# A graph network's relation passes: one gather for each tile of edges, with staging by ScalarE, in place of one gather for each step

## The chip, the cores and the metric

The kernel runs on one core of a Trainium2 chip. The metric is the device time of one execution in microseconds (us). Before the change it was 3381.78 us, the median of three runs (3381.7, 3381.78 and 3384.83 us).

## The reference

Four graph networks run one after the other over the same 3125 nodes (128 features) and 100,000 edges, each with a residual and a layer norm. The edges come sorted by destination. The change touches the last one, a relational network with two layers and 8 relations:

```python
def rgcn_layer(x, src, dst, etype, W, W_root, b, num_rels):
    N = x.shape[0]
    h = jnp.einsum('ni,rio->rno', x, W)
    msg = h[etype, src]
    seg = dst * num_rels + etype
    sums = jax.ops.segment_sum(msg, seg, num_segments=N * num_rels)
    cnt = jax.ops.segment_sum(jnp.ones(msg.shape[0], x.dtype), seg, num_segments=N * num_rels)
    mean = sums / jnp.maximum(cnt, 1.0)[:, None]
    agg = mean.reshape(N, num_rels, W.shape[-1]).sum(axis=1)
    return agg + x @ W_root + b

h = jax.nn.relu(rgcn_layer(x, src, dst, edge_type, W1, root1, b1, 8))
y = rgcn_layer(h, src, dst, edge_type, W2, root2, b2, 8)
x = layernorm(x + y)
```

## The kernel before

The instructions are written out by hand for each engine; every engine runs its own list in order and meets the others by semaphores. There is no scheduler, so the order of the code is the order on the engine.

**Tiles, windows and steps.** The 100,000 sorted edges are cut into T = 782 tiles of 128 edges, one edge for each partition. The destinations are cut into windows of 64 nodes (WR = 64), 49 of them. A tile whose edges belong to two windows must be worked on twice, once for each, so a pass over all edges has JR = 782 + 49 - 1 = 830 steps: each step is one (tile, window) pair, and most tiles have one step, 48 of them one more.

**The plan (the first 94 us).** The kernel finds at run time which tile and which window a step has. DVE makes masks (L1162, from what ACT wrote in L786) of the steps that belong to a tile, PE multiplies tables of the edges with the masks (L444), and the result in PSUM is the table for the steps: source, relation, destination, tile. This is done in four chunks of up to 512 steps: two for the adjacency matrix (977 steps with windows of 16 nodes), two for the relation passes (512 and 318 steps). `expand` on DVE (L1080 to L1155) turns each chunk into indices, codes and windows. SP writes those of the relation passes to DRAM (L371 to L373) and reads them back later (L389 to L391). After the plan DVE waits for these writes (L1169) and clears a part of the adjacency matrix (L1170), and the building of that matrix begins (L464 on PE, L1177 on DVE). PE gets leave for it from SP, in a loop over gates that reads its numbers from SBUF into registers, 32 at a time (L377 to L384).

**The adjacency matrix and the three networks before (94 to 1060 us)** are not touched.

**The two relation passes.** Pass 0 (L655, `scatter(0)`) sums rows of `table1`, the node features, pass 1 (L668) rows of `table2`, which the stage between the passes makes. In each of the 830 steps of a pass
- POOL issues one indirect DMA (L739), which gathers 128 rows of 256 half-precision numbers (each value as a high and a low half) into one of NG = 6 buffers `gath`. It waits for the step 6 before to be done on PE (`scattered`);
- DVE makes a one-hot matrix 128x512 of the edges' (node, relation) codes (L1459), 4 steps ahead;
- PE multiplies the one-hot matrix with the gathered rows: 12 matmuls (L584, L587) into one of 3 pairs of PSUM banks. It waits for the gather's semaphore, for the one-hot matrix, and for the pair of banks;
- DVE adds the pair of banks into `sums` at the window of the step, whose number it has in a register (L1475). Every 32 steps it reads 32 windows into registers (L1469).

SP and ACT do nothing in a pass, but for work on weights in pass 0: four squares on ACT at its beginning (L934 to L937), products on PE, reductions on DVE, and three more instructions on ACT (L940 to L945).

**Between the passes** the sums are scaled and go through both layers' weights (25 blocks), POOL clears `sums` block by block (L750), and SP writes `table2`. After pass 1 the slots are scaled and placed (L682), and the last norm follows.

In the profile's rows most tiles of the passes carry the name `adj`: they lie in the space of the adjacency matrix.

## Time and profile before

| | |
|---|---|
| median of 3 runs | 3381.78 us |
| the profiled execution's own time | 3388.58 us |
| its span | 3386.7 us |
| PE busy | 2448.9 us (72%) |
| DVE busy | 2483.4 us (73%) |
| POOL busy | 1985.1 us (59%) |
| ACT busy | 509.9 us (15%) |

The profile is of one execution; its own time is 6.8 us above the median of the runs, and 1.9 us of it lie outside the span. A busy share is an average over stages with different limits, so what counts is which wait ends last in a stage. Of the span, each of the two relation passes takes 1040 us, the stage between them 193 us, the plan 94 us, and the rest, up to pass 0, 966 us.

### The profile page before, as it was taken

How to read it: one execution, taken by the hardware profiler on the slowest of the kernel's cores; microseconds unless marked ns; L12 is line 12 of the kernel's file. 1: busy time of each engine (PE TensorE's matmuls, PEld its weight loads, DVE VectorE, ACT ScalarE, POOL GpSimd, SP SyncE). 2: the span in 40 equal slices, each digit the busy share in tenths (PEclk: the TensorE clock that was granted, in tenths of full speed). 3: DMA queues.
4: the chain of work that ended last, by engine and by line, in shares of the span. 5: the costliest groups of instructions: out<-in, count | busy, mean ns of one | idle time of the engine just before them, and what ended most of it. 6: DMA issues, size and time to landing. Idle time of an engine off the chain costs nothing.

```text
span 3386.7 us, 73088 instructions
## 1 busy us (share of the span) xinstructions
PE 2448.9 (72%) x27967; PEld 1801.3 (53%) x27967; DVE 2483.4 (73%) x6336; ACT 509.9 (15%) x989; POOL 1985.1 (59%) x2158
## 2 busy tenths in 40 slices
PE   4677778998994766666666666996666666676667
PEld 1222255557443555555555555775555555565556
DVE  5999983556416877777777777667777777777777
ACT  2455552116112000000000000550000000000003
POOL 1788840000006777777777776116777777777776
PEclk9889898998997999999999999998999999999999
DMA  1000000000011222222222221112222222222221
GB/s 42 16 1 1 1 6 2 1 1 2 1 39 48 53 54 53 54 54 54 54 54 54 54 54 45 70 76 60 54 53 54 54 53 54 53 54 54 54 54 40
DMA packets 76149, 138.75 MB, mean 41 GB/s; under 512 B 29902, under 2 KB 44640, under 8 KB 75810
## 3 DMA queue, kind: packets, MB, share of 16 engines
q0 software_dynamic: 53120, 108.90, 12.3%
q1 hardware_dynamic: 18934, 24.46, 2.1%
q8 instruction: 231, 3.78, 0.5%
q10 hardware_dynamic: 3756, 0.73, 0.2%
q14 instruction: 108, 0.88, 0.1%
HBM read 116.35 MB, written 17.62 MB: 40 GB/s over the span
## 4 chain that ended last, share of the span: by engine, by line
PE 32%; DMA 25%; POOL 17%; DVE 14%; issue 8%; ACT 2%; ACTq 1%; SPq 0%; DVEq 0%; POOLq 0%
DMA adj<-table,adj 25%; POOL adj L739 17%; PE banks L584 8%; DVE hi_hot L1177 7%; PE banks L516 6%; PE banks L509 3%; PE banks L587 3%; DVE lo_hot L1185 3%; PE banks L631 2%; PE banks L643 2%; PE banks L491 1%; PE banks L682 1%; PE banks L495 1%; ACT adj L822 1%; PE banks L616 1%
## 5 line engine op out<-in xcount | busy, mean ns | idle before, releaser
L584 PE MATMUL banks<-adj 128*128 128x129 f16 x13280 | 1412.9, 226 | 697.7 <-DMA adj<-table,adj 683.8
L739 POOL DMA_INDIRECT adj<-table,adj x1660 | 1574.7, 949 | 538.5 <-PE banks L584 316.2
L584 PEld LDWEIGHTS banks<-adj 128*128 128x128 f16 x13280 | 1077.1, 100 | 924.8 <-DMA adj<-table,adj 910.7
L1475 DVE TENSOR_TENSOR adj<-adj,banks 128x516 f32 x1660 | 1147.4, 691 | 460.6 <-PE banks L584 423.0
L587 PE MATMUL banks<-adj 128*128 128x127 f16 x6640 | 1248.6, 224 | 0.0
L587 PEld LDWEIGHTS banks<-adj 128*128 128x128 f16 x6640 | 672.4, 101 | 1.3 <-issue 1.0
L1459 DVE TENSOR_SCALAR adj<-adj 128x512 f16<-128x512 f16 x1660 | 642.9, 388 | 0.0
L713 POOL TENSOR_SCALAR lo_hot<-minus_iota,zT 128x128 f16<-128x128 f16 x392 | 323.5, 842 | 134.6 <-PE banks L464 72.6
L464 PE MATMUL banks<-hi_hot,lo_hot 128*128 128x400 f16 x977 | 269.6, 383 | 114.6 <-DVE hi_hot L1177 75.2
L1177 DVE TENSOR_SCALAR hi_hot<-iota,zT 128x400 f16<-128x400 f16 x977 | 271.0, 340 | 7.1 <-PE banks L464 6.7
L720 POOL MEMSET adj<- 128x1548 f16 x1 | 1.4, 1388 | 468.2 <-PE banks L516 468.2
L464 PEld LDWEIGHTS banks<-hi_hot,lo_hot 128*128 128x128 f16 x977 | 101.8, 104 | 282.3 <-issue 228.7
L516 PE MATMUL banks<-adj,split 128*128 128x512 f16 (+1 forms) x1190 | 235.7, 356 | 0.0
L996 ACT ACTIVATE adj<-adj 128x128 f32<-128x128 f32 x75 | 22.0, 392 | 1050.2 <-DVE adj L1487 1050.2
L516 PEld LDWEIGHTS banks<-adj,split 128*128 128x128 f16 x1190 | 109.6, 98 | 117.3 <-issue 2.9
L956 ACT ACTIVATE adj<-banks 128x512 f16<-128x512 f32 x50 | 26.9, 585 | 940.3 <-PE banks L616 940.3
L509 PE MATMUL banks<-adj,split 128*128 128x512 f16 (+1 forms) x560 | 115.4, 370 | 25.0 <-DVE split L1268 20.2
L809 ACT ACTIVATE adj<-banks 128x400 f16<-128x400 f32 x196 | 98.7, 503 | 185.1 <-PE banks L464 184.3
L1185 DVE TENSOR_SCALAR lo_hot<-minus_iota,zT 128x128 f16<-128x128 f16 x585 | 119.8, 279 | 0.0
L750 POOL MEMSET adj<- 128x1032 f32 x25 | 24.0, 959 | 153.6 <-PE banks L616 153.6
L509 PEld LDWEIGHTS banks<-adj,split 128*128 128x128 f16 x560 | 53.0, 101 | 86.6 <-issue 20.4
L1315 DVE SCALAR_TENSOR_TENSOR zT<-banks,dinv,rows 128x128 f32<-128x128 f32 x75 | 21.2, 342 | 97.8 <-PE banks L533 97.6
(229 smaller groups left out, 1811.7 us busy)
## 6 DMA issues: line engine op xcount, KB each, us to landing
adj<-table,adj POOLq DMA_INDIRECT x1660
table<-adj SPq DMA_DIRECT2D x25, 512.0 KB, 2.6
table<-split SPq DMA_DIRECT2D x6, 256.0 KB, 2.3
out_dram<-xres SPq DMA_DIRECT2D x6, 256.0 KB
adj<-in_L_gnn_W_dram SPq DMA_DIRECT2D x1, 1024.0 KB, 7.4
adj<-in_L_gnn_W_dram SPq DMA_DIRECT2D x2, 512.0 KB, 9.1
adj<-scr_index SPq DMA_DIRECT2D x1, 830.0 KB
scr_index<-adj SPq DMA_DIRECT2D x1, 512.0 KB
```

The source lines that it names most:

```text
L464: e.matmul(banks[:, bass.ds(c, 1), 0:NC].rearrange("p o n -> p (o n)"), lo_hot[:, g % NLO, j % LG, :], hi_hot[:, j % NHI, :], start=False, ...
L509: e.matmul(bank[c][:, 0:n], split[:, k, s, :], adj[:, k, c0:c0 + n], start=(k == 0 and s == 0), stop=False)
L516: m = e.matmul(bank[c][:, 0:n], split[:, k, s, :], adj[:, k, c0:c0 + n], start=False, stop=(k == NB - 1 and s == 1))
L584: m = e.matmul(ps[:, g * CH // 2:g * CH // 2 + b - a], hot[:, s, g * P:g * P + P], gath[:, s, a:b], start=(q == 0), stop=(q == 1), skip_gr ...
L587: e.matmul(ps[:, g * CH // 2 + D + 1:(g + 1) * CH // 2], hot[:, s, g * P:g * P + P], gath[:, s, 0:CH // 2 - D - 1], start=True, stop=True, ...
L713: e.tensor_scalar(lo_hot[:, g % NLO, k, :], minus_iota[:, :], nlo[:, j:j + 1], None, ALU.is_equal).then_inc(low_pool, 1)
L739: e.indirect_dma_start(gath[:, s, 0:2 * D], None, table, bass.IndirectOffsetOnAxis(ap=index[:, which, j:j + 1].bitcast(U32), axis=0)).then ...
L809: e.activation(adj[:, :, w * WA:(w + 1) * WA], v.rearrange("p (h n) -> p h n", n=WA), ACT.Copy).then_inc(evicted, 1)
L1177: e.tensor_scalar(hi_hot[:, j % NHI, :], iota[:, :], code[:, j:j + 1], None, ALU.is_equal).then_inc(high, 1)
L1185: e.tensor_scalar(lo_hot[:, g % NLO, j % LG, :], minus_iota[:, :], nlo[:, j:j + 1], None, ALU.is_equal).then_inc(low_dve, 1)
L1459: e.tensor_scalar(hot[:, s, :], iota_r[:, :], code_r[:, j:j + 1], None, ALU.is_equal).then_inc(hot_set, 1)
L1475: e.tensor_tensor(a, a, ps[:, :].rearrange("p (g d) -> p g d", g=G)[:, :, 0:D + 1], ALU.add).then_inc(accumulated, 1)
```

## The change

A pass gathers each tile once, 782 gathers, and still has 830 steps. The buffers are now 16 (`gath`, NG = 16) and belong to tiles. A step's rows come to PE by way of a second set of 6 buffers (`edge`), into which ACT copies the tile of the step; which tile that is it reads from a register (`tile_regs`, 32 at a time). SP runs a loop over the tiles in each pass (`relay`): it waits for the gathers in order and counts them in `landed`, for which ACT waits, and it tells POOL (`slot_free`) which buffers are free: those of tiles whose last step ACT has copied, a number that SP too reads into registers (`last_regs`). The one-hot matrices keep 6 buffers. The three instructions on ACT in pass 0 are put between its copies, and DVE's work on the second layer's weights begins 14 steps later.

In the plan, the index tables need only one column for each tile: PE turns the table of edges (35 small matmuls at its beginning), ACT writes them out, and SP sends them to DRAM once. So `expand` for the relation chunks loses three DVE instructions of each chunk and gets a small one (the row of tiles), and PE's product for a tile and chunk has 4 matmuls in place of 6. DVE makes the row of last steps from `ends` (2 small instructions).

POOL fills `place` after pass 0, not before it, and `place` lies in memory of its own.

```diff
+LEAD = 8
-        NG = 6
+        NG, NSTG, NHOT = 16, 6, 6
-        gath = carve([P, NG, D + 1], F16)
-        hot = carve([P, NG, G * P // 2], F16)
+        gath = carve([P, NG, D], F16)
+        edge = carve([P, NSTG, D + 1], F16)
+        hot = carve([P, NHOT, G * P // 2], F16)
-        index = carve([P, 2, JR], I32)
+        index = carve([P, 2, T], I32)
-                   {0: [S_LO, S_HI], 1: [TYPE], 2: [D_LO[1], D_HI[1]], 3: [TILE]})
+                   {1: [TYPE], 2: [D_LO[1], D_HI[1]], 3: [TILE]})
# SP
+            e.wait_ge(index_set, 3)
+            e.dma_start(scr_i, out_i[:, :, :]).then_inc(last_out, 16)
...
+            def relay(which):
+                for t in range(T):
+                    u = t + LEAD - NG
+                    if u >= 0 and t + LEAD < T:
+                        if u % REGS == 0:
+                            n = min(REGS, T - NG - u)
+                            e.load(last_regs[0:n], last_row[:, u:u + n])
+                        e.reg_alu(least, last_regs[u % REGS], 1, ALU.max)
+                        e.wait_ge(staged_edges[which], least)
+                        e.sem_inc(slot_free[which], 1)
+                    e.wait_ge(gathered[t % NG], 16 * (which * (-(-(T - t % NG) // NG)) + t // NG + 1))
+                    e.sem_inc(landed[which], 1)
# PE, at its beginning
+            for b in range(TB):
+                rws = P if b < TFULL else TLAST
+                at = slice(b % 4 * P, b % 4 * P + rws)
+                for q in (S_LO, S_HI):
+                    e.matmul(bank[4 + b // 4][:, at], piece[0:rws, q, b, :], ident16[0:rws, 0:rws],
...
# PE, scatter
-                    e.wait_ge(gathered[s], 16 * uses)
+                    e.wait_ge(staged_edges[which], j + 1)
# POOL
             def gather(which, table):
-                base = which * JR
-                for j in range(JR):
-                    s = j % NG
-                    if base + j >= NG:
-                        e.wait_ge(scattered, base + j - NG + 1 if j >= NG else base)
+                if which:
+                    e.wait_ge(staged_edges[0], JR)
+                for t in range(T):
+                    s = t % NG
+                    if t >= NG:
+                        e.wait_ge(slot_free[which], t - NG + 1)
                     e.indirect_dma_start(
-                        gath[:, s, 0:2 * D], None, table,
-                        bass.IndirectOffsetOnAxis(ap=index[:, which, j:j + 1].bitcast(U32), axis=0)).then_inc(gathered[s], 16)
+                        gath[:, (t + 1) % NG, :], None, table,
+                        bass.IndirectOffsetOnAxis(ap=index[:, which, t:t + 1].bitcast(U32), axis=0)).then_inc(gathered[s], 16)
# ACT
+            def stage_edges(which):
+                base = which * JR
+                for j in range(JR):
+                    if j % REGS == 0:
+                        n = min(REGS, JR - j)
+                        e.load(tile_regs[0:n], tile_row[:, j:j + n])
+                    e.reg_alu(least, tile_regs[j % REGS], 1, ALU.max)
+                    e.wait_ge(landed[which], least)
+                    if base + j >= NSTG:
+                        e.wait_ge(scattered, base + j - NSTG + 1)
+                    c = e.snap(tile_regs[j % REGS], min_val=1, max_val=T) % NG
+                    e.activation(edge[:, j % NSTG, 0:2 * D], gath[:, bass.ds(c, 1), :].rearrange("p o f -> p (o f)"),
+                                 ACT.Copy).then_inc(staged_edges[which], 1)
+                    if which == 0 and j >= REGS:
+                        between(j - REGS)
# DVE, expand for a relation chunk
-                    e.tensor_copy(out_i[:, 0, 0:n], sets[0][:, 0:n]).then_inc(own_dve, 1)
-                    e.tensor_copy(Y, sets[1][:, 0:n]).then_inc(own_dve, 1)
...
-                    e.scalar_tensor_tensor(out=out_i[:, 1, 0:n], in0=sets[0][:, 0:n], scalar=float(REL), in1=Y,
-                                           op0=ALU.mult, op1=ALU.add).then_inc(sums_read, 1)
+                    e.tensor_scalar(rows_i[:, 1, 0:n], sets[3][0:1, 0:n], 1.0, None, ALU.add).then_inc(own_dve, 1)
```

How the instructions move. POOL's list from the sums' clearing to the end of pass 1, before (`table` is the gathered table, `adj 128x25800` the clearing of `sums`):

```order
L731 MEMSET adj 128x25800
L739 DMA adj<-table,adj 128x256 [waits table1_out,rel_set,list_in]
L739 DMA adj<-table,adj 128x256 x5
L739 DMA adj<-table,adj 128x256 [waits scattered] x824
L750 MEMSET adj 128x1032 [waits row_turned] x25
L739 DMA adj<-table,adj 128x256 [waits scattered,table2_out1,table2_out0]
L739 DMA adj<-table,adj 128x256 [waits scattered] x829
```

and now:

```order
L778 MEMSET adj 128x25800
L787 DMA adj<-table,adj 128x256 [waits table1_out,rel_set,list_in]
L787 DMA adj<-table,adj 128x256 x15
L787 DMA adj<-table,adj 128x256 [waits slot_free0] x766
L798 MEMSET adj 128x1032 [waits row_turned] x25
L800 MEMSET place 128x1024
L804 COPY place<-ident 64x4x64 [waits own_pool]
L804 COPY place<-ident 64x4x64 [waits place_set] x3
L787 DMA adj<-table,adj 128x256 [waits table2_out1,staged_edges0,table2_out0,place_set]
L787 DMA adj<-table,adj 128x256 x15
L787 DMA adj<-table,adj 128x256 [waits slot_free1] x766
```

A pass has 782 gathers in place of 830; what they wait for comes from SP, and `place` is filled between the passes.

ACT's list at the beginning of pass 0, before (the squares, the three instructions on bounds and weights, then the first block between the passes):

```order
L934 ACTIVATE zT<-adj 128x2304 [waits table1_out,l3_in]
L935 ACTIVATE h<-colp 128x2
L936 ACTIVATE zT<-adj 128x256
L937 ACTIVATE w1p<-adj 128x2048
L940 ACTIVATE bound<-bound 128x4 [waits bound_set]
L942 ACTIVATE w1p<-adj,scales 128x2304 [waits scale_set]
L945 ACTIVATE adj<-adj,scales 128x2304 [waits w_low]
L956 ACTIVATE adj<-banks 128x8x64 [waits row_turned,w_low]
```

and now:

```order
L1024 ACTIVATE zT<-adj 128x2304 [waits table1_out,l3_in]
L1025 ACTIVATE h32<-colp 128x2
L1026 ACTIVATE zT<-adj 128x256
L1027 ACTIVATE w1p<-adj 128x2048
L999 TENSOR_LOAD rows [waits list_in]
L1000 REGISTER_ALU
L1004 ISA [waits landed0]
L1005 ACTIVATE adj<-adj 128x256
L1000 REGISTER_ALU
L1004 ISA [waits landed0]
L1005 ACTIVATE adj<-adj 128x256
```

A step on ACT is three instructions, a register's maximum, one that takes the buffer's number and carries the wait, and the copy of 128x256; a load of registers stands ahead of every 32 steps.

DVE's list for the first relation chunk (512 steps) in the plan, before:

```order
L1097 SCALAR_TENSOR_TENSOR adj<-adj 128x512 [waits own_dve]
L1139 CAST adj<-banks 128x512
L1141 COPY adj<-banks 128x512
L1144 SCALAR_TENSOR_TENSOR adj<-banks,adj 128x512 [waits own_dve]
L1148 SCALAR_TENSOR_TENSOR adj<-banks,adj 128x512 [waits own_dve]
L1151 SCALAR_TENSOR_TENSOR adj<-adj 128x512 [waits own_dve]
L1153 TENSOR_SCALAR adj<-adj 128x512 [waits own_dve]
L1155 CAST adj<-adj 1x512
L1162 TENSOR_SCALAR adj<-adj 128x318 [waits picked_abs] x2
```

and now:

```order
L1188 SCALAR_TENSOR_TENSOR adj<-adj 128x512 [waits own_dve]
L1230 TENSOR_SCALAR adj<-banks 1x512
L1232 SCALAR_TENSOR_TENSOR adj<-banks,adj 128x512
L1236 SCALAR_TENSOR_TENSOR adj<-adj 128x512 [waits sums_read,own_dve]
L1238 TENSOR_SCALAR adj<-adj 128x512 [waits own_dve]
L1240 CAST adj<-adj 1x512
L1247 TENSOR_SCALAR adj<-adj 128x318 [waits picked_abs] x2
```

Three instructions on 128 partitions are gone, one on a single partition is new.

## Rows read from the trace of the kernel before

**Rows 1.** Busy time by stage; columns are named in the first row.

```profile
core 0: us, PE busy (x) PEld busy (x) DVE busy (x) ACT busy (x) POOL busy (x), PEclk, DMA share, GB/s
1060.49:2100.69 1040.20, 703.80 (x9966) 584.65 (x9966) 815.08 (x1700) 8.13 (x7) 787.40 (x830) 0.98 0.21 54
2100.69:2293.47 192.78, 181.18 (x2049) 143.94 (x2049) 122.78 (x207) 91.41 (x200) 23.96 (x25) 0.98 0.18 70
2293.47:3333.56 1040.09, 713.00 (x9936) 604.45 (x9936) 809.56 (x1658) 0.00 (x0) 787.31 (x830) 0.95 0.21 54
```

**Rows 2.** Waits on POOL: waiter, releaser, us in total, times, longest.

```profile
POOL adj L739 <- PE banks L584: 316.2, 1037, 0.3
POOL adj L739 <- issue: 189.4, 621, 0.3
```

**Rows 3.** POOL in order of time: start, us, what, idle before.

```profile
1019.22 1.77 POOL L727 COPY adj<-ident 64x256 f32<-64x256 f32 x4
...
1060.49 1.30 POOL L739 DMA_INDIRECT adj<-table,adj  x1 [17.70 <-DMA table<-split]
...
2099.69 1.00 POOL L739 DMA_INDIRECT adj<-table,adj  x1 [0.30 <-PE banks L584]
...
2277.25 0.96 POOL L750 MEMSET adj<- 128x1032 f32 x1 [6.09 <-PE banks L616]
2293.47 1.71 POOL L739 DMA_INDIRECT adj<-table,adj  x1 [15.26 <-DMA table<-adj]
```

**Rows 4.** One line of code each: ns min/median/max, first and last start.

```profile
L739 POOL DMA_INDIRECT adj<-table,adj x1660: 941/947/1712, 1060.5 to 3332.6; - x185
L1459 DVE TENSOR_SCALAR adj<-adj x1660: 336/349/598, 1057.9 to 3331.9; 128x512 f16<-128x512 f16 x185
L971 ACT ACTIVATE hTp<-h x25: 416/416/417, 2117.8 to 2284.2; 128x256 f16<-128x256 f32 x25
```

**Rows 5.** PE, its first matmul of pass 0, in order of time.

```profile
1063.38 0.29 PE L584 MATMUL banks<-adj 128*128 128x129 f16 x1 [29.87 <-DMA adj<-table,adj]
```

**Rows 6.** The chain that ended last: the longest landing in it.

```profile
2900.57 4.39 DMA adj<-table,adj
```

**Rows 7.** DVE behind a late landing, in order of time.

```profile
3328.56 0.69 DVE L1475 TENSOR_TENSOR adj<-adj,banks 128x516 f32 x1 [1.43 <-PE banks L584]
...
3329.47 0.69 DVE L1475 TENSOR_TENSOR adj<-adj,banks 128x516 f32 x1
```

**Rows 8.** DVE at step 32 of pass 0, where it loads 32 registers.

```profile
1105.63 0.69 DVE L1475 TENSOR_TENSOR adj<-adj,banks 128x516 f32 x1 [1.45 <-issue]
```

**Rows 9.** ACT in the plan, in order of time.

```profile
74.16 0.56 ACT L786 ACTIVATE adj<-adj 128x318 f16<-128x318 f16 x1 [6.27 <-PE banks L444]
76.83 0.56 ACT L786 ACTIVATE adj<-adj 128x318 f16<-128x318 f16 x1 [2.11 <-PE banks L444]
```

**Rows 10.** DVE in the plan, the relation chunks, in order of time.

```profile
79.90 0.68 DVE L1139 CAST adj<-banks 128x512 int32<-128x512 f32 x1
80.50 0.68 DVE L1141 COPY adj<-banks 128x512 f32<-128x512 f32 x1
...
83.35 0.41 DVE L1155 CAST adj<-adj 1x512 int32<-1x512 f32 x1
...
87.65 0.49 DVE L1139 CAST adj<-banks 128x318 int32<-128x318 f32 x1
...
93.83 0.72 DVE L1170 MEMSET adj<- 128x800 uint32 x1 [3.52 <-DMA scr_windows<-adj]
```

**Rows 11.** PE in the plan, its last product and the first of the next stage.

```profile
84.03 1.90 PE L444 MATMUL banks<-adj 128*128 128x318 f16 x12 [1.52 <-DVE adj L1162]
99.32 1.18 PE L464 MATMUL banks<-hi_hot,lo_hot 128*128 128x400 f16 x3 [13.39 <-SPq L383]
```

**Rows 12.** SP's last write of the plan.

```profile
91.55 0.32 SPq L373 DMA_DIRECT2D scr_windows<-adj  x1
```

**Rows 13.** The last add of pass 0 on DVE.

```profile
2103.98 0.69 DVE L1475 TENSOR_TENSOR adj<-adj,banks 128x516 f32 x1 [1.22 <-PE banks L584]
```

More of the change, by code:

```diff
@@ L402, in _ @@
                             split[:, q0:q1, :, :].rearrange("p b q d -> p b (q d)")).then_inc(table1_out, 16)
+            last_regs = [e.alloc_register(f"last_use{i}") for i in range(REGS)]
+            def relay(which):
[10 more added lines that the diff above has]
+                    e.sem_inc(landed[which], 1)
+            e.wait_ge(list_in, 80)
+            relay(0)
             for nb in range(NB):
@@ L930, in _, with between @@
                 split_high(xres, quad, FX)
+            tile_regs = [e.alloc_register(f"tile{i}") for i in range(REGS)]
+            def stage_edges(which):
[13 more added lines that the diff above has]
+                        between(j - REGS)
+            def between(t):
+                if t == 34:
+                    e.wait_ge(bound_set, 6)
+                    e.activation(bound[:, 12:16], bound[:, 8:12], ACT.Sqrt).then_inc(bound_root, 1)
+                elif t == 38:
+                    e.wait_ge(scale_set, 1)
+                    e.activation(w1p[:, 0, :, :].rearrange("p r o -> p (r o)"), w1[:, :], ACT.Identity,
+                                 scale=scales[:, 0, 0:1]).then_inc(w_high, 1)
+                elif t == 54:
+                    e.wait_ge(w_low, RR)
+                    e.activation(w2p[:, 0, :, :, :], w2_r[:, :, :, :], ACT.Identity, scale=scales[:, 0, 2:3]).then_inc(w_high, 1)
             e.wait_ge(l3_in, 16 * (3 + HB))
```

123 lines of the change are left out of this document (77 added, 46 removed).

## The prediction

> **What bounds the kernel now.** I read the busy time by stage first, then the waits of the engine whose instructions fill the passes, then that engine in order of time. By stage [rows 1] the two relation passes are 1040.20 and 1040.09 us, 61% of the span. In them no engine is full: DVE is busy 78%, POOL 76%, PE 68%. The chain of waits there goes back and forth between landings, POOL and PE, and names no bound. The waits on POOL do [rows 2]: 1658 of its 1660 gathers are preceded by an idle of at most 0.3 us, whoever is named as its releaser. So POOL never waits for a buffer; it issues a gather, takes 0.30 us, and issues the next. The gather itself is 947 ns in the median [rows 4]. Over a pass that is 1040.15 / 830 = 1.2532 us for each gather, first start to last end [rows 1, 3]. POOL's rate of issue is the bound, and everything behind it (landing, PE, DVE) follows with slack: when a landing is late, DVE's next add comes 0.91 us after the one before [rows 7], which is what a step costs DVE if nothing is missing.
>
> **Fewer gathers.** A pass issues 782 in place of 830, so 2 x 48 x 1.2532 = **-120.3 us**, if POOL still never waits and a gather costs the same. Both must be shown for the new cover.
>
> *Does POOL wait for SP?* Gather t waits for SP's round t - 8, which begins once tile t - 9 has landed. From the end of gather t - 9 to the start of gather t there are 8 x 1.25 + 0.30 = 10.3 us. A landing takes 1.6 us (first gather's end 1061.79 to the first matmul at 1063.38) [rows 3, 5] and at the worst in the chain 4.4 us [rows 6]. So SP and the copies behind have 5.9 to 8.7 us before POOL stands still. A round also waits for the last step of tile t - 16, which lies a further 8 tiles back.
>
> *Do the steps keep up?* They must now do 830 steps in 782 x 1.2532 = 980 us, 1.181 us each. DVE: 830 x 0.91 = 755 us if no mask is ever long, and at most the 815 us that it was busy in pass 0, weights included [rows 1]; with 26 loads of registers at 1.45 us [rows 8], at most 853 us. ACT: a copy of 128x256 is 416 ns [rows 4]; the nearest dearer row, 128x318 with a bias, is 560 ns [rows 9]. The two register instructions ahead of it I bound by DVE's, which fit with two computing instructions into 0.91 us; so a step is 0.42 to 0.91 us, I take 0.6, and with the loads ACT needs 540 us of 980. ACT's two large weight instructions fall between copies, but ACT was busy 8.1 us in all in pass 0 [rows 1], and the steps catch up 0.2 us a step. PE was busy 704 of 1040 us. SP's round is four semaphore operations and a register operation; by the same DVE row it is under 0.91 us. None reaches 980, so POOL stays the bound, and DVE, at 853, is next.
>
> *A rule against it.* The row first: the gather's duration has 941 ns as its least and 947 as its median, while the mask on DVE goes from 336 to 598 ns [rows 4]; where the two meet, it is DVE that becomes longer. The Trainium skill (SBUF — State Buffer, Who interferes with whom and the box on the trap that DVE blocks DMA) says that a DVE copy or tensor-scalar instruction in a two-port mode locks out POOL, which then cannot write its descriptors until the instruction ends. By that rule the denser masks would stretch each gather (the first rival below); by the row they do not. I go by the row.
>
> **The plan.** PE's product for a tile of the first relation chunk loses 2 of 6 matmuls. ACT's masks follow it 2.67 us apart [rows 9], so the last two that DVE waits for come 2 x 2.67 / 3 = 1.8 us sooner. DVE loses three instructions at 0.60 us and gets one like the 0.34 us of a single-partition row (83.35 to 83.69, start to start; 0.41 alone): -1.5 [rows 10]. The 318-step chunk: PE 12 matmuls in 1.90 us become 8, -0.6 [rows 11]; DVE three at about 0.4, one more at 0.3, -0.9. Two small instructions of DVE before the masks, at most 0.41 each [rows 10], cost about 0.4. Sum **-4.4 us**. PE's 35 matmuls and ACT's two writes are done while DVE still prepares the masks (PE has no other work before DVE's first masks, by the program's order); should they not be hidden, they cost a few us. The other end: DVE waits 3.52 us for the last write [rows 10], which is shorter now without the indices, so down to -8; upwards 0, if PE is bound by something else there.
>
> **Ends of the passes.** After the last gather's end (2100.69) the last add is over at 2104.67 [rows 3, 13], 4.0 us. Now a hop over SP and a copy lie in between: 0.42 for the copy and I take 0.4 for the semaphores, **+1.6 us** for both passes. Bounds: 0.8, and by the longest answer of SP that any row shows (its last write ends at 91.87, PE's gate opens at 99.32, 7.4 us [rows 11, 12]) about 16.
>
> **At nothing.** The squares on ACT (part of its 8.1 us) delay the first copies, not POOL, which has 16 free buffers, 20 us. Filling `place` costs POOL a memset of about 1 us and 1.77 us of copies [rows 3], now after the last clearing at 2277.25; the gather behind it waits until 2293.47 for `table2`, so 15.3 us hide it. Before pass 0 POOL was waiting 17.7 us anyway, so nothing is gained there. SP's writes of the indices go out while SP is idle.
>
> **Sum.** -120.3 - 4.4 + 1.6 = -123.1 us. Against the profiled execution's 3388.58 us that is 3265.5; against the median of the runs, 6.8 us lower, 3258.7. I predict **3259 us**.
>
> **Rivals.**
>
> *The mask lock.* If POOL stands still while a mask is made, a gather contains the mask's time today, and with 830/782 masks for each gather it grows by 0.349 x 48/782 = 0.021 us [rows 4]. 1564 x 0.021 = 34: **3293 us**. For it: the rule. Against: the gather's constant duration [rows 4]. 8%.
>
> *The step, not the gather, carries the 1.253 us* (the change doesn't give what it says): the new chain of SP, ACT, PE and back through buffers takes as long for a step as a gather does now. Then both passes stay at 1040 us: 3381.8 - 4.4 + 1.6 = **3379 us**. Against: the 0.91 us [rows 7] and 6 buffers on each side. 5%.
>
> *Slower: loads of registers stop the relay.* SP and ACT now each load 32 registers every 32 tiles or steps, and during SP's load no landing is told on. DVE's load costs 1.45 us [rows 8]; the only row with SP's is the 7.4 us before the first gate [rows 11, 12], which held one load. If SP's and ACT's both cost 7.4 us and follow each other, that is 14.9 us of standstill in 32 tiles, beyond POOL's slack; with their 34 steps at DVE's 815 / 830 = 0.98 us, 32 tiles take 14.9 + 33.3 = 48.2 us, a pass (24.4 such stretches) 1177 us, and the kernel 3381.8 - 2.8 + 2 x 137 = **3653 us**. It makes the kernel slower from a standstill of 1040.15 / 24.4 - 33.3 = 9.3 us in 32 tiles; a load of 7.4 us alone would nearly be hidden (40.7 us where POOL needs 40.1). For: the relay is a single chain. Against: DVE was at its clearing until 94.55 there [rows 10] and made PE's next masks after it, so much of the 7.4 us need not be SP's. 6%, with milder forms of it in between at 3270 to 3320 us, 3%.
>
> **How the numbers follow.** The forecast has 78%, with its own range 3248 to 3272 (the plan's 0 to -8, the ends' bounds, 0.2% for the runs). A time within 0.2% of before (6.8 us) can't be told from no change. Faster: 78 + 8 + 3 = 0.89. Same: 0.05. Slower: 0.06. The range 3245 to 3300 takes in the lock.
>
> **What the profile after would show.** Right: 782 gathers in a pass, idle 0.30 us before nearly each, first start to last end 980 us; 830 copies on ACT of about 0.42 us; DVE busy about 83% of a pass; the plan's clearing on DVE at about 89.5 instead of 93.83 us; the stage between the passes still 193 us. Wrong: gathers longer than 0.95 us in the median (the lock); idle before gathers released by SP (the relay), in bursts every 32 tiles (the loads); steps at a regular 1.25 us with ACT or PE full. The forecast would also fall if TensorE's granted clock, 0.98 and 0.95 in the passes [rows 1], sank for long: at the lower of its two levels, 1.2 GHz, the 12 matmuls of a step with 128 columns each are 1.28 us, more than the 1.18 us there are.

## The result, and the profile after

The changed kernel takes 3261.51 us (median of 4 runs, 3260.66 to 3262.88) against 3382.28 us (4 runs, 3381.7 to 3384.83) for the kernel before on the same chip: ratio 0.9642, 95% interval 0.963 to 0.9653. Predicted were 3259 us, with 3245 to 3300 as the range. The profiled execution's own time is 3260.66 us, its span 3258.8 us, 127.9 us less than before. The medians differ by 120.8 us; the traced execution of before was 6.3 us above its median, so some of the 127.9 us below are not the change's.

Busy time by stage, after. The stages are the plan (from DVE's first cast to its clearing), the untouched part, pass 0, the stage between, and pass 1; rows two to four answer to [rows 1].

```profile
core 0: us, PE busy (x) PEld busy (x) DVE busy (x) ACT busy (x) POOL busy (x), PEclk, DMA share, GB/s
1052.01:2033.19 981.18, 690.58 (x9948) 594.49 (x9949) 792.79 (x1698) 339.00 (x835) 743.04 (x782) 0.97 0.19 54
2033.19:2224.38 191.19, 180.13 (x2069) 143.20 (x2067) 124.61 (x210) 92.24 (x202) 26.44 (x30) 0.97 0.17 70
2224.38:3205.15 980.77, 679.89 (x9930) 579.96 (x9931) 784.14 (x1658) 332.70 (x828) 742.64 (x782) 0.98 0.19 54
24.37:87.34 62.97, 36.12 (x168) 16.84 (x168) 45.69 (x109) 23.47 (x38) 8.89 (x12) 0.88 0.06 20
87.34:1052.01 964.67, 774.74 (x5531) 413.89 (x5531) 643.12 (x2505) 357.75 (x650) 340.08 (x385) 0.91 0.02 7
```

Both passes lost 59 us and still run at POOL's rate: 981.18 / 782 = 1.2547 and 980.77 / 782 = 1.2542 us for each gather, where it was 1.2532. The waits of the engines, after (waiter, releaser, us in total, times, longest):

```profile
POOL adj L787 <- issue: 443.6, 1455, 0.3
POOL adj L787 <- SPq L436: 32.6, 107, 0.3
ACT adj L1005 <- SPq L438: 1005.1, 1048, 7.1
ACT adj L1005 <- PE banks L637: 236.2, 238, 2.4
ACT adj L1005 <- issue: 50.3, 71, 0.9
PE banks L637 <- ACT adj L1005: 585.8, 908, 30.4
```

1562 of the 1564 gathers start after at most 0.3 us of idle, whoever is named, as in [rows 2]. ACT waits for SP to report a landing and PE for ACT: the relay waits for gathers, not gathers for the relay. One line of code each (ns min/median/max), against [rows 4]:

```profile
L787 POOL DMA_INDIRECT adj<-table,adj x1564: 941/947/1296, 1052.0 to 3204.2; - x196
L1005 ACT ACTIVATE adj<-adj x1660: 398/417/420, 1055.4 to 3207.6; 128x256 f16 x185
L1545 DVE TENSOR_SCALAR adj<-adj x1660: 334/349/593, 1049.4 to 3203.9; 128x512 f16<-128x512 f16 x185
L433 SPq TENSOR_LOAD <-rows x48: 1860/1864/2077, 1063.7 to 3159.0; - x48
L999 ACTq TENSOR_LOAD <-rows x52: 1945/1964/2200, 1051.3 to 3170.4; - x52
```

The last two are the loads of 32 registers on SP and on ACT: 1.86 and 1.96 us each.

The span's difference, piece by piece (start of one row to start or end of another, in both traces):

| piece | before | after | difference | predicted |
|---|---|---|---|---|
| to DVE's first cast (waits for inputs) | 26.03 | 24.37 | -1.66 | 0 |
| first cast to the plan's clearing | 67.80 | 62.97 | -4.83 | -4.4 |
| clearing to first gather | 966.66 | 964.67 | -1.99 | 0 |
| pass 0 | 1040.20 | 981.18 | -59.02 | -60.2 |
| between the passes | 192.78 | 191.19 | -1.59 | +0.8 |
| pass 1 | 1040.09 | 980.77 | -59.32 | -60.2 |
| after the last gather | 53.14 | 53.65 | +0.51 | +0.8 |

### The profile page after: what moved, and what is told of

Its sections match the earlier page's. It is cut to its first block, busy times and chain, and to the rows that moved or that the text cites. A ratio compares the mean times of both kernels' runs of the same rounds, so it can differ in the third digit from the quotient of the medians.

```text
span 3258.8 us, 84381 instructions
## 1 busy us (share of the span) xinstructions
PE 2400.5 (74%) x27974; PEld 1786.4 (55%) x27974; DVE 2433.1 (75%) x6334; ACT 1176.6 (36%) x2651; POOL 1898.6 (58%) x2063
## 3 DMA queue, kind: packets, MB, share of 16 engines
q1 hardware_dynamic: 19354, 24.37, 2.1%
## 4 chain that ended last, share of the span: by engine, by line
POOL 38%; PE 20%; issue 13%; DVE 13%; DMA 8%; SPq 2%; ACT 2%; DVEq 0%; ACTq 0%; POOLq 0%
POOL adj L787 37%; DMA adj<-table,adj 8%; DVE hi_hot L1263 7%; PE banks L571 6%; PE banks L564 4%; DVE lo_hot L1271 3%; PE banks L684 2%; PE banks L696 2%; SPq L433 2%; PE banks L546 1%; POOL lo_hot L767 1%; PE banks L735 1%; PE banks L550 1%; ACT adj L882 1%; PE banks L669 1%
## 5 line engine op out<-in xcount | busy, mean ns | idle before, releaser
L637 PE MATMUL banks<-adj 128*128 128x129 f16 x13280 | 1368.7, 224 | 624.2 <-ACT adj L1005 585.8
L787 POOL DMA_INDIRECT adj<-table,adj x1564 | 1485.7, 950 | 511.9 <-issue 443.6
L640 PE MATMUL banks<-adj 128*128 128x127 f16 x6640 | 1226.6, 222 | 0.0
L1005 ACT ACTIVATE adj<-adj 128x256 f16 x1660 | 665.6, 415 | 1294.1 <-SPq L438 1005.1
L1545 DVE TENSOR_SCALAR adj<-adj 128x512 f16<-128x512 f16 x1660 | 611.7, 369 | 0.0
L872 ACT ACTIVATE banks<-banks 128x400 f32<-128x400 f32 x188 | 91.7, 488 | 6.0
```

What stands on the lines that cost most here:

```text
L637: m = e.matmul(ps[:, g * CH // 2:g * CH // 2 + b - a], hot[:, j % NHOT, g * P:g * P + P], edge[:, j % NSTG, a:b], start=(q == 0), stop=(q ...
L640: e.matmul(ps[:, g * CH // 2 + D + 1:(g + 1) * CH // 2], hot[:, j % NHOT, g * P:g * P + P], edge[:, j % NSTG, 0:CH // 2 - D - 1], start=Tr ...
L787: e.indirect_dma_start(gath[:, (t + 1) % NG, :], None, table, bass.IndirectOffsetOnAxis(ap=index[:, which, t:t + 1].bitcast(U32), axis=0)) ...
L1005: e.activation(edge[:, j % NSTG, 0:2 * D], gath[:, bass.ds(c, 1), :].rearrange("p o f -> p (o f)"), ACT.Copy).then_inc(staged_edges[which], 1)
L1545: e.tensor_scalar(hot[:, s, :], iota_r[:, :], code_r[:, j:j + 1], None, ALU.is_equal).then_inc(hot_set, 1)
```

## The experiments

They ran on four chips, and these are of two kinds. On two of them the kernel before takes 3805.43 and 3803.41 us, not 3382; its stages up to 1060 us are as usual there and only the relation passes are longer. On these ran the runs with fewer gathers (both), short masks, half rows, eight pieces, the changed kernel again, the plan back and the weights moved. The others (four pieces, short loads, eight buffers, SP's increments) ran on two chips like the first one (kernel before 3389.29 us in a single run, and 3391.23 us). A time is compared with a kernel's on the same kind of chip.

**Fewer gathers, nothing else** (kernel before).

```diff
+        def left_out(j):
+            return j % 17 == 16 and j < 816
...
                     s = j % NG
+                    if left_out(j):
+                        continue
                     if base + j >= NG:
...
-                    uses = which * (-(-(JR - s) // NG)) + j // NG + 1
-                    e.wait_ge(gathered[s], 16 * uses)
+                    mine = [i for i in range(s, JR, NG) if not left_out(i)]
+                    uses = which * len(mine) + sum(i <= j for i in mine)
+                    if not left_out(j):
+                        e.wait_ge(gathered[s], 16 * uses)
```

> The kernel before, with 48 of the 830 gathers of each pass left out (every 17th step multiplies whatever rows lie in its buffer, so the sums of those steps are wrong); no relay on SP, no copies on ACT, 6 buffers, 830 steps. Theory (POOL's rate of issue is the bound): a pass has 782 gathers at 1.2532 us, 980 us, and the kernel is 3382.3 - 120.3 = 3262 us. Rival (a step, whatever is gathered for it, carries 1.25 us): both passes stay at 1040 us and the kernel at 3382 us. Its distance to the changed kernel (3261.5 us, with a plan shorter by some 5 us) is what relay and copies cost: under the theory less than 2 us beside the plan.

Measured: 3674.19 us against 3805.43, ratio 0.9652 (0.9636 to 0.9668), -131 us; the passes 1180.48 and 1182.54 us. Run again on another such chip:

> The kernel before, with 48 gathers of each pass left out (the steps 16, 33, 50 and so on use what stands in the buffer); no other edit. Theory (POOL's rate of issue is the bound and nothing else of the change matters): 2 x 48 x 1.253 = 120 us less than before, 3262 us, both passes at 980 us, and idle before the gathers still 0.30 us. Rival (the steps carry part of the time, and the new buffers and copies were needed for the gain): the passes stay above 1000 us, with idle before the gathers released by PE.

Measured: 3671.49 us against 3803.41, ratio 0.9652 (0.9637 to 0.9666); passes 1181.00 and 1179.48 us. On both chips leaving out 48 gathers in a pass takes 66 us from it (1247.62 in the kernel with moved weights, below), 1.4 us each, though POOL does wait there: its waits, second run,

```profile
POOL adj L746 <- PE banks L589: 476.4, 447, 1.8
POOL adj L746 <- issue: 334.1, 1062, 2.8
```

POOL waits for PE here, and the passes stay above 1000 us, which were the rival's signs; so on this chip the run doesn't show that POOL's rate of issue is the bound. Nor does a step have a price of its own: with the same 830 steps the pass became shorter, and it is 1247.62 / 830 = 1.503 us for each gather with all gathers and 1181.00 / 782 = 1.510 with fewer. Late landings don't hold up PE there. In the kernel with moved weights (830 gathers, same kind of chip, below) PE waits 48.0 us for them in both passes, 30.2 of it for the first one, where it waited 683.8 us in the trace of before:

```profile
PE banks L585 <- DMA adj<-table,adj: 48.0, 17, 30.2
```

What the run does show is that fewer gathers shorten the passes without the new buffers and copies. 3262 us could not be tested on this chip.

**Masks of 2 columns in place of 512** (changed kernel; the one-hot matrices keep old contents).

```diff
-                e.tensor_scalar(hot[:, s, :], iota_r[:, :], code_r[:, j:j + 1], None, ALU.is_equal).then_inc(hot_set, 1)
+                n = G * P if base + j < NHOT else 2
+                e.tensor_scalar(hot[:, s, 0:n], iota_r[:, 0:n], code_r[:, j:j + 1], None, ALU.is_equal).then_inc(hot_set, 1)
```

> The changed kernel with DVE's mask made whole only for the first 6 steps; from then on the instruction writes 2 of its 512 columns, so PE multiplies old masks (wrong sums). Theory: the gather's duration does not depend on DVE's masks, it stays at 947 ns in the median, a pass at 981 us and the kernel at 3260 us. Rival (a mask on DVE holds up POOL's descriptors and a gather contains its 0.35 us): gathers fall towards 0.6 us and a pass towards 830 x 0.75 us, the rate of PE and DVE's adds, the kernel below 3000 us.

Measured: 3903.01 us, passes 1288.01 and 1283.73 us; this is the slower kind of chip, so only the durations of single instructions answer. The groups of the two lines (busy us, mean ns | idle before):

```profile
L787 POOL DMA_INDIRECT adj<-table,adj x1564 | 1476.6, 944 | 1131.0 <-SPq L436 719.2 <-issue 376.0 <-DMA table<-split 23.0
L1546 DVE TENSOR_SCALAR adj<-adj 128x2 f16<-128x2 f16 x1654 | 378.3, 229 | 0.0
```

The changed kernel has 359 and 956 ns on such a chip (below). The mask fell by 130 ns; if a gather held a mask's time, it would have fallen by as much, and it fell by 12, or by 4 against fewer gathers, which has whole masks and 948 ns. The lock isn't what a gather's time consists of. That the pass would fall with it couldn't be seen here, as POOL waits for SP.

**Half of each row** (256 bytes for each partition in place of 512; the low halves are not gathered).

```diff
-                        gath[:, (t + 1) % NG, :], None, table,
+                        gath[:, (t + 1) % NG, 0:D], None, table.rearrange("n (h d) -> (n h) d", h=2),
```

> The changed kernel with 256 bytes gathered for each row in place of 512, from wrong places (the index is not doubled), so the sums are wrong. Theory: a gather costs POOL by its 128 rows, not its bytes: 947 ns, a pass 981 us, 3261 us. Rival (the gather's bytes or the transfer are the bound): a gather's time falls with the bytes, to 0.5 to 0.7 us, and DVE becomes the bound at about 850 us a pass, 3000 us.

Measured: 3904.15 us on the same chip, passes 1282.01 and 1281.15 us, gathers 954 ns in the mean (changed kernel below: 1285.29, 1270.69, 956). Half the bytes change nothing, neither in the gather nor in the pass: POOL's 0.95 us are for issuing, not for moving.

**ACT's copy in eight pieces, then in four** (changed kernel; the four differ only in the numbers).

```diff
-                    e.activation(edge[:, j % NSTG, 0:2 * D], gath[:, bass.ds(c, 1), :].rearrange("p o f -> p (o f)"),
-                                 ACT.Copy).then_inc(staged_edges[which], 1)
+                    for q in range(8):
+                        m = e.activation(edge[:, j % NSTG, q * 32:q * 32 + 32],
+                                         gath[:, bass.ds(c, 1), q * 32:q * 32 + 32].rearrange("p o f -> p (o f)"),
+                                         ACT.Copy)
+                    m.then_inc(staged_edges[which], 1)
```

> The changed kernel with ACT's copy of 256 columns cut into 8 instructions of 32 columns. Nothing is left out. Two copies of ACT follow each other 0.30 us apart in the trace of the changed kernel; 8 short ones should take 1.2 to 2.0 us with the step's register work. Theory: a step's work on ACT is free up to 1.18 us and binds beyond it: at 1.6 us a pass is 830 x 1.6 = 1330 us and the kernel 3960 us, POOL idle before its gathers and released by SP. Rival (ACT's copies are never on the path, only landings are): 3261 us.

Measured: 4015.38 us, passes 1344.54 and 1340.29 us, where the changed kernel has 1285.29 and 1270.69 on such a chip (below): 59 and 70 us more. The pieces overlap: ACT was busy 936.37 us of pass 0, 1.13 us a step, not the 1.6 us that the expectation took, so its 1330 us for a pass was met by luck, on a chip where the pass has 1285 us without the pieces.

> The changed kernel with ACT's copy of 256 columns cut into 4 instructions of 64 columns, which should take ACT 0.8 to 1.0 us a step in place of 0.42. Nothing is left out. Theory (a step has 1.18 us, and ACT's work is beside the path): the two passes stay at 981 us, but for some 0.4 us more at the end of each; 3262 us. Rival (the copy is a link of the chain that sets the pace of a step): 0.5 us more for each of 1660 steps, 4090 us.

Measured, on a chip like the first: 3259.82 us (one run), passes 978.90 and 977.72 us. Pass 0 with four pieces, and POOL's waits:

```profile
1054.52:2033.42 978.90, 693.49 (x9954) 598.97 (x9954) 795.24 (x1698) 567.87 (x3319) 740.87 (x782) 0.96 0.22 55
```

```profile
POOL adj L787 <- issue: 442.2, 1451, 0.3
POOL adj L787 <- SPq L436: 33.8, 111, 0.3
```

ACT's busy time in a pass grew by 229 us and the pass by nothing. So the copy was hidden, as forecast, with at least that much to spare on this kind of chip.

**Registers 8 at a time**, on SP and ACT, in place of 32 (changed kernel).

```diff
+SHORT = 8
-                        if u % REGS == 0:
-                            n = min(REGS, T - NG - u)
+                        if u % SHORT == 0:
+                            n = min(SHORT, T - NG - u)
...
-                    if j % REGS == 0:
-                        n = min(REGS, JR - j)
+                    if j % SHORT == 0:
+                        n = min(SHORT, JR - j)
```

> The changed kernel with registers loaded 8 at a time instead of 32, by SP's relay and by ACT: 4 times as many loads, 98 and 104 a pass. Nothing is left out. Theory: a load stops relay or copies by about 1.4 us as on DVE, POOL's slack of 6 to 9 us covers each, and 8 tiles take 10.0 us where the steps need 8.3 us and the loads 1.4 or twice that: 3262 us, at most 3330 us if both loads add up. Rival (the loads are of the 7.4 us kind): 8 tiles would take 16 us, over 4000 us.

Measured: 3266.95 us (one run), passes 984.05 and 984.08 us. Four times as many loads bring 3 us to a pass. But a load of 8 registers is shorter, 0.52 us on SP, so that SP's loads grew only from 24 x 1.86 = 45 us to 96 x 0.52 = 50 us in a pass; the run tests more stops, not longer ones. SP's loads, ACT's waits and POOL's, here:

```profile
L434 SPq TENSOR_LOAD <-rows x192: 520/523/736, 1063.2 to 3194.9; - x192
ACT adj L1006 <- issue: 180.7, 241, 0.9
POOL adj L788 <- issue: 452.9, 1486, 0.3
POOL adj L788 <- SPq L437: 23.2, 76, 0.3
```

ACT's idle that is released by nothing rises from 50.3 to 180.7 us, yet POOL still waits 0.3 us at most. What lengthened the passes is the mean of a gather, 954 ns in place of 950 (1564 x 0.004 = 6 us in all), which also lies among the other runs' 944 to 956. The slower rival's standstill is not there, and its 7.4 us a load are refuted by the loads' own rows (1.86 and 1.96 us for 32 registers, above).

**8 buffers with a lead of 4** in place of 16 and 8 (changed kernel).

```diff
-LEAD = 8
+LEAD = 4
-        NG, NSTG, NHOT = 16, 6, 6
+        NG, NSTG, NHOT = 8, 6, 6
```

> The changed kernel with 8 buffers for tiles in place of 16, and SP's answer 4 tiles ahead in place of 8. Nothing is left out. Theory: POOL's slack for a late landing falls from 5.9 us to 0.9 us and for an ordinary one to 3.7 us, so POOL waits rarely: 3261 to 3275 us, idle before gathers of more than 0.3 us only behind late landings or loads. Rival (16 buffers are what made the gain): the passes lose most of it, 3300 to 3380 us.

Measured: 3267.26 us (one run), passes 983.98 and 982.63 us, gathers 953 ns, POOL's longest idle 0.3 us. Half the buffers would do on this chip.

**The changed kernel again.**

> The changed kernel once more, beside the others of this job, as the measure for them. If the first measurement holds on this chip, 3261 us against 3382 us (ratio 0.964), with 981 us for each pass. The rival for the chip on which the first four experiments ran: if this one's kernel before is at 3805 us again, the changed kernel shows by how much a program with more instructions (84,381 in place of 73,088) suffers there; a slow supply of instructions would put it near 3900 us and over 1.28 us for each gather, although a gather lasts 0.95 us.

Measured: 3893.04 us (5 runs, 3886.61 to 3897.22) against 3803.41 us (15 runs): ratio 1.0236, interval 1.0222 to 1.025. **On this chip the change makes the kernel slower.** By stage (the two passes), the kernel with moved weights (830 gathers) first, fewer gathers next, the changed kernel last:

```profile
1058.25:2305.87 1247.62, 804.15 (x9946) 683.60 (x9947) 831.18 (x1695) 8.13 (x7) 790.30 (x830) 0.89 0.17 45
2498.16:3744.69 1246.53, 794.62 (x9917) 677.37 (x9918) 818.99 (x1653) 0.00 (x0) 790.93 (x830) 0.89 0.17 45
```

```profile
1060.42:2241.42 1181.00, 790.56 (x9950) 673.79 (x9950) 824.68 (x1696) 8.13 (x7) 741.25 (x782) 0.89 0.17 45
```

```profile
1056.27:2341.56 1285.29, 815.62 (x9761) 713.17 (x9762) 767.63 (x1663) 315.30 (x821) 747.85 (x782) 0.84 0.16 41
2549.36:3820.05 1270.69, 809.42 (x9720) 710.58 (x9720) 758.98 (x1619) 310.92 (x813) 747.61 (x782) 0.83 0.16 42
```

Waits of the changed kernel there:

```profile
POOL adj L787 <- SPq L436: 689.7, 498, 5.1
ACT adj L1005 <- PE banks L637: 1516.2, 895, 4.6
PEld banks L637 <- issue: 584.5, 896, 16.9
```

The gather is as cheap as ever (956 ns in the mean), but POOL waits 690 us for SP, SP for ACT, ACT for PE. So the chain through the steps sets the pace, 1285.29 / 830 = 1.55 us for a step. PE's rows in order of time show how a step comes late there:

```profile
1502.24 0.22 PE L637 MATMUL banks<-adj 128*128 128x129 f16 x1 [1.62 <-issue]
...
1505.15 0.22 PE L637 MATMUL banks<-adj 128*128 128x129 f16 x1 [2.06 <-ACT adj L1005]
...
1507.04 0.42 PE L637 MATMUL banks<-adj 128*128 128x128 f16 x2
```

In these rows PE idles 1.6 and 2.1 us between two steps, the first time with no releaser; behind the second stop, from 1506.3 to 1509.7 us, the granted clock is at its lower level (1.2 GHz), and two matmuls take 0.42 us where they take 0.28 at the upper (2.4 GHz). The mean over the pass is 0.84 in place of 0.97. Against fewer gathers alone the changed kernel pays 104 + 91 us in the passes, and 13 + 17 us where it must still work off the tiles that POOL is ahead (207.8 us between the passes in place of 194.7, 71.2 us behind the last gather in place of 54.2); 4 us come back in the plan and the stage behind it. Together 221 us, which turn -132 into +90.

The beginning of a pass shows the stops at their plainest. While POOL fills its free buffers, one gather every 1.25 us, the others nearly stand still. The first three rows of PE are the last matmuls of one step, which wait for no semaphore; the fourth begins the next step and waits for an add of DVE's, whose products PE had finished before 1064 us:

```profile
1069.80 0.27 PE L637 MATMUL banks<-adj 128*128 128x129 f16 x1 [1.89 <-issue]
1071.21 0.27 PE L640 MATMUL banks<-adj 128*128 128x127 f16 x1 [1.14 <-issue]
1072.60 0.27 PE L637 MATMUL banks<-adj 128*128 128x128 f16 x1 [1.12 <-issue]
...
1088.97 0.27 PE L637 MATMUL banks<-adj 128*128 128x129 f16 x1 [16.10 <-DVE adj L1561]
```

```profile
1084.14 0.95 POOL L787 DMA_INDIRECT adj<-table,adj  x1 [0.30 <-issue]
1087.54 0.94 POOL L787 DMA_INDIRECT adj<-table,adj  x1 [2.46 <-SPq L436]
1088.13 0.69 DVE L1561 TENSOR_TENSOR adj<-adj,banks 128x516 f32 x1 [20.77 <-remote]
1088.21 0.42 ACT L1005 ACTIVATE adj<-adj 128x256 f16 x1 [19.58 <-remote]
```

DVE, ACT and PE go on within 0.9 us of each other, 3 us after POOL's last gather in the row has ended at 1085.09.

From one add on DVE to the next it is 21.7 us here, with 16 gathers in it, and 17 to 22 us at the beginning of each pass in all five traces of the changed kernel and its variants on these chips. On the first kind of chip the longest such distance there is 3.5 us, and in the kernel before, where POOL can be only 6 gathers ahead, 4.3 us on these chips. Together with the constant 1.50 to 1.51 us for each gather above, this suggests, and doesn't prove, that on these chips the other engines are held up while POOL issues gathers, and the longer, the further POOL may run ahead. It was not tested: the run with 8 buffers was on a chip where nothing stops.

**The sources' tables back in the plan** (changed kernel).

```diff
-                    {1: [TYPE], 2: [D_LO[1], D_HI[1]], 3: [TILE]})
+                    {0: [S_LO, S_HI], 1: [TYPE], 2: [D_LO[1], D_HI[1]], 3: [TILE]})
...
+                    e.tensor_copy(Y, sets[0][:, 0:n]).then_inc(own_dve, 1)
+                    own.up()
+                    e.wait_ge(own_dve, own.n)
+                    e.tensor_copy(Y, sets[1][:, 0:n]).then_inc(own_dve, 1)
+                    own.up()
                     e.tensor_scalar(rows_i[:, 1, 0:n], sets[3][0:1, 0:n], 1.0, None, ALU.add).then_inc(own_dve, 1)
+                    own.up()
+                    e.wait_ge(own_dve, own.n)
+                    e.scalar_tensor_tensor(out=GE, in0=sets[0][:, 0:n], scalar=float(REL), in1=Y,
+                                           op0=ALU.mult, op1=ALU.add).then_inc(own_dve, 1)
```

> The changed kernel with the sources' tables back in the plan: PE makes 6 matmuls for each tile and relation chunk in place of 4, and DVE again does the three instructions on 128 partitions of each chunk (their result is not used). Theory of the prediction: the clearing on DVE, 62.97 us after its first cast now, comes 4.4 to 4.8 us later, at 67.4 to 67.8, and the kernel takes 4 to 5 us more than the changed one, near 3265.5 us. Rival (DVE's wait for the last write, 2.30 us now, takes up what is added, or ACT's masks set the pace): under 2 us.

Measured: first cast to clearing 26.37 to 95.26, 68.89 us, where the changed kernel beside it has 26.45 to 90.52, 64.07: +4.82 us. The time is 3899.41 us against 3893.04, +6.4, which its runs' spread (3886.88 to 3901.82) can't tell from less. The second chunk with the instructions back, PE's product and DVE, in order of time; last PE's product in the changed kernel:

```profile
84.40 3.47 PE L499 MATMUL banks<-adj 128*128 128x318 f16 x12 [4.19 <-DVE adj L1256]
87.91 0.49 DVE L1179 SCALAR_TENSOR_TENSOR adj<-adj,banks 128x318 f32<-128x318 f32 x1 [3.35 <-PE banks L499]
...
95.26 0.72 DVE L1265 MEMSET adj<- 128x800 uint32 x1 [2.30 <-issue]
```

```profile
80.03 1.36 PE L499 MATMUL banks<-adj 128*128 128x318 f16 x8 [1.02 <-DVE adj L1247]
```

The wait ahead of the clearing is 2.30 us with and without them, so it takes up nothing. But the 4.82 us are not the forecast's terms put back. DVE's two chunks take 2.04 and 1.43 us more, the second product makes DVE wait 2.1 us more, and DVE begins the first chunk 0.8 us sooner than in the changed kernel beside it. The granted clock is part of that: the second product ran at 0.50 here and its 12 matmuls took 3.47 us, where the same 12 took 1.90 at 1.00 in the trace of before [rows 11], and the first ran at 1.00 (42 matmuls in 7.04 us; 11.13 at 0.62 before).

**The weights moved by 8 bytes** (kernel before).

```diff
+        carve([P, 2])
         w1 = carve([P, RR * H])
```

> The kernel before, with its two tables of weights w1 and w2 moved on by 8 bytes in each partition, so that they begin at a multiple of 32 bytes as in the changed kernel; nothing else. Between the passes the changed kernel needs 6.93 us for a block in place of 7.05, though none of its instructions there are changed. Theory (the addresses are the cause): 6.93 us a block, 190 us between the passes in place of 193, the kernel 3 us shorter, 3379 us. Rival (the cause is another, as the clock or what else is in memory): 7.05 us a block as before, no change of the time.

Measured: 3800.05 us against 3803.41, ratio 0.9994 (0.9985 to 1.0003), which settles nothing by itself; but 192.29 us between the passes, where fewer gathers has 194.68 on this chip, and a block in 6.93 us in place of 7.05. One group of PE's in a block (54 matmuls, their moving operand in the memory of `w2`), first of the kernel before, then moved:

```profile
2244.81 3.30 PE L631 MATMUL banks<-adj,w1p 128*128 128x128 f16 x54
```

```profile
2346.31 3.18 PE L632 MATMUL banks<-adj,w1p 128*128 128x128 f16 x54
```

On the moved weights' own chip the group takes 3.30 us in fewer gathers, so the chip is not what differs. 0.12 us for 54 matmuls is the whole difference of a block, and 25 blocks make 3.0 us (2.4 in the stage as a whole). The addresses are the cause.

**4100 semaphore increments on SP in pass 0** (kernel before).

```diff
+            e.wait_ge(gathered[0], 16)
+            for i in range(4100):
+                e.sem_inc(gate, 1)
             for nb in range(NB):
```

> The kernel before, with 4100 semaphore increments that nobody waits for on SP, begun when the first gather of pass 0 has landed; pass 1 is left as it is and serves as the measure. It asks what the mere number of instructions costs that the changed kernel gives to SP and ACT. Theory A (the engines' instructions come over something that they share, and it is this supply that runs short on the chip on which the kernel before takes 3805 us): on that chip the changed kernel has about 5600 more instructions in a pass and pays 290 - 200 = 90 to 105 us more for pauses, 16 to 19 ns each, so 4100 of them cost 65 to 80 us and pass 0 takes 1312 to 1325 us where pass 1 takes 1247; on a chip on which the kernel before takes 3382 us nothing, as the changed kernel there has no pauses: 1040 us for both. Theory B (what matters is which instructions they are, ACT's copies and the chain through them, not their number): both passes alike on either chip, 1247 or 1040 us, and the kernel's time that of before within 0.2%.

Measured, on a chip like the first: 3391.37 us against 3391.23, ratio 1.0001 (0.9991 to 1.0011); passes 1041.52 and 1040.42 us. There the number of instructions costs nothing, as both theories have it; the chip on which they differ was not met again.

## Why the prediction was right

*The bound.* POOL's rate of issue, from 830 gathers at 1.2532 us: the changed passes are 782 gathers at 1.2547. Of the predicted -120.3 us came -118.3; the 1.3 ns that a gather takes more in the mean of both passes are 2.0 us. On this kind of chip it rests on the trace itself (at most 0.3 us of idle before 1658 of 1660 gathers [rows 2] and now before 1562 of 1564) and on the runs with four pieces, short loads and 8 buffers, which leave it alone. That masks and bytes have no part in a gather's 0.95 us was measured on the other kind, on single gathers.

*The cover.* POOL doesn't wait for SP (0.3 us at most, and still so with half the buffers). ACT's copy is 417 ns (416 was taken); ACT was busy 339 us of a pass. A load of 32 registers, for which DVE's 1.45 us was taken, is 1.86 us on SP and 1.96 on ACT, still within POOL's slack. DVE is busy 81% of a pass, 83% was forecast. The landings in the chain have 4.68 us as their longest; 4.39 was the row's [rows 6].

*The plan.* -4.4 predicted, -4.83 measured, and that they lie so close is in part luck. By the starts of DVE's rows in both traces, DVE reaches the first relation chunk 1.33 us sooner (forecast -1.8 + 0.4), spends 1.01 us less on it (-1.5), waits 0.54 us less for the second product (-0.6) and spends 0.73 us less on the second chunk (-0.9): -3.6 together. The other 1.22 us are the wait for the last write, 2.30 us in place of 3.52 [rows 10], which the forecast named as a way down to -8 and left out of its sum. The +4.82 when undone is made of other parts, the clock's among them (above). The clearing came at 87.34 us, not 89.5, partly because DVE's first cast came 1.66 us earlier; in the traces of all kernels that cast lies between 24.4 and 28.0 us, so this is scatter of the input's landing. The row of tiles is the term that was mis-sized: 0.60 us from start to start where 0.34 was taken (0.67 alone; its source is PSUM, that of the 0.41 us row is not). PE's turning ran from 28.52 to 32.1 us, before ACT's masks, at nothing.

*The ends.* +0.8 for each was forecast. From the last gather's end to the last add's it is 2033.19 to 2037.80, 4.61 us in place of 3.98 [rows 3, 13], so +0.6.

*At nothing.* `place` is filled behind the last clearing, and POOL still waits 12.87 us for `table2` afterwards:

```profile
2207.83 0.96 POOL L798 MEMSET adj<- 128x1032 f32 x1 [5.97 <-PE banks L669]
2208.73 0.95 POOL L800 MEMSET place<- 128x1024 f32 x1
2209.74 1.77 POOL L804 COPY place<-ident 64x256 f32<-64x256 f32 x4
2224.38 1.28 POOL L787 DMA_INDIRECT adj<-table,adj  x1 [12.87 <-DMA table<-adj]
```

*What was missed.* The stage between the passes was to stay; it is 1.59 us shorter although its end carries the +0.6: the new buffers moved the weights' addresses. The 1.99 us of the untouched stage stay open; kernels that are alike there differ by as much (961.6 to 968.7 us).

*The rivals.* The mask lock is refuted by the gather's 944 ns without masks and by the pass at 981 us with them; the Trainium skill (SBUF — State Buffer, Who interferes with whom) has it that a DVE instruction in a two-port mode blocks GpSimd for its whole length, and no trace here shows it for the mask beside an indirect DMA. The step that carries the time is refuted on the first kind of chip. On the second its signs are there (the passes don't get shorter, POOL waits), but a fixed price of a step is not: the same 830 steps took 66 us less a pass with fewer gathers, and more with the new chain. A load of 32 registers is at most 2.2 us on ACT and 2.1 on SP, not 7.4, and SP's never stopped POOL there.

*What the prediction didn't have.* Its last sentence named a sunken clock as what would make it fall. On another kind of chip a step costs 1.50 us in the old form and 1.55 in the new, the clock is at 0.89 and 0.84, and the change loses 2.4% (measured on one such chip; on the other, two variants took 3903 and 3904 us against 3805). So the forecast holds for the kind of chip whose trace it was read from, which is also where the result was measured; for another kind it had no term. What stops the engines there is open. Against a lack of bytes or a slow gather stand the gathers' durations (944 to 956 ns everywhere), the run with half rows, and PE's 48 us of waits for landings. For the gathers themselves, as what holds up the others, speak the standstill at the beginning of each pass and the 1.50 to 1.51 us for each gather. For the supply of instructions, which may itself be what the gathers hold up, speak idle times with no releaser, in the middle of a step too, and the 59 to 70 us that eight pieces cost; but those could also be ACT's own time (busy 1.13 us of a step's 1.62), and the experiment made to tell them apart ran where neither shows. Whether the clock falls because PE stops, or the stops are the clock's, was not separated either. Stops come first in the rows shown; between the passes, where PE is busy over 90% of the time, the clock is 0.96 to 0.98 on both kinds of chip; and from the first kind of chip to the second the changed kernel's pass 0 rose by 304 us and PE's busy time in it by 125, so matmuls at the lower clock are not the whole of it.

## What to carry to other kernels

Where an engine that issues indirect DMAs goes from one to the next with the same short idle, its count times its step is the stage's time. Leaving some of the DMAs out of the old kernel shows the most that a change can gain, but not what its cover costs: on the slower chips that was -132 us where the change itself gave +90. Such a gain is worth what the next bound leaves: here DVE was busy 81% of a pass and PE 70% on one chip, and on another the steps themselves were late, so a change that trades issues for longer chains of instructions should be timed on more than one. Undo a part and read its stage in the trace: 4.8 us are plain there, where the total can't show them. Then read it piece by piece, with the granted clock beside it, before taking a matching sum for a matching cause.

## What the runs showed of the hardware

- An indirect DMA of 128 rows keeps POOL for 944 to 956 ns in the mean and is followed by 0.30 us where POOL has nothing to wait for, with rows of 512 or of 256 bytes, with long or short masks on DVE, on either kind of chip.
- Chips differ by 12% on one program (3382 to 3391 us on some, 3803 and 3805 on two), and, by the traces of moved weights and of fewer gathers, only in the relation passes, which are some 20% longer there (1247 in place of 1040 us).
- On the slower chips, at the beginning of a pass with 16 free buffers, DVE's adds stop for 17 to 22 us while POOL issues 11 to 16 gathers; on the others for 3.5 us at most.
- A load of 32 registers is 1.86 us on SP and 1.96 on ACT, one of 8 registers 0.52 on SP.
- 54 matmuls of 128 columns take 3.30 us with their moving operand in one place and 3.18 us 8 bytes on (2.2 ns each).
- A copy of 128x64 on ACT is 240 ns in the median, one of 128x256 417 ns.
- 4100 semaphore increments on SP beside a pass cost it nothing (1041.52 us, where the pass without them in the same run has 1040.42).
